# Summing both parts of the attention scores in PSUM as 128-column products, with one clip on VectorE

## The reference

```python
q = (lat @ Wq).reshape(b, n, HEADS, DHEAD).transpose(0, 2, 1, 3)
k, v = jnp.split(ctx @ Wkv, 2, axis=-1)
k = apply_rope(k, cos[None, None], sin[None, None])
attn = jnp.einsum('bhnd,bhsd->bhns', q, k) * DHEAD ** (-0.5)
attn = jnp.clip(attn, -11.0, 11.0)
attn = jax.nn.softmax(attn, axis=-1)
out = jnp.einsum('bhns,bhsd->bhnd', attn, v)
```

## Time and profile before

| | us |
|---|---|
| median of 3 runs | 1478.19 (1476.39 to 1479.28) |
| the profiled execution | 1474.36 |
| its span | 1472.6 |
| TensorE busy | 1385.8 (94%) |
| VectorE, ScalarE, GpSimd busy | 849.3, 792.9, 844.1 |

### The profile page before, as it was taken

One profiled execution on the slowest core, in us unless ns is written; L12 is line 12 of the kernel. 1 busy time (PEld: TensorE's weight loads), 2 busy tenths in 40 slices (PEclk: granted clock), 3 DMA queues, 4 the chain that ended last, 5 costly groups with the idle time before them and its releaser, 6 DMA issues. The chain is left out here.

```text
span 1472.6 us, 25163 instructions
## 1 busy us (share of the span) xinstructions
PE 1385.8 (94%) x8732; PEld 1137.1 (77%) x8732; DVE 849.3 (58%) x1417; ACT 792.9 (54%) x1224; POOL 844.1 (57%) x727
## 2 busy tenths in 40 slices
PE   4899999999999999999999999999995899999993
PEld 2578888888888888878888888888885576866662
DVE  7366665666556566656665666565553456665552
ACT  2346566656566666656566656666554212445650
POOL 3457777766677777767677767777665233200002
PEclk9999999999999999999999999999996899899997
DMA  6567666766667766657666766667566650569983
GB/s 209 205 108 133 122 119 111 131 116 135 123 108 128 118 129 112 132 109 125 122 117 128 116 134 120 122 117 119 88 103 147 231 213 0 195 241 360 359 322 107
DMA packets 115236, 218.44 MB, mean 148 GB/s; under 512 B 13328, under 2 KB 49168, under 8 KB 108944
## 3 DMA queue, kind: packets, MB, share of 16 engines
q1 hardware_dynamic: 111648, 208.48, 63.2%
q0 software_dynamic: 1280, 4.20, 0.9%
q10 hardware_dynamic: 2160, 3.93, 0.7%
HBM read 132.67 MB, written 16.78 MB: 101 GB/s over the span
## 5 line engine op out<-in xcount | busy, mean ns | idle before, releaser
L572 POOL TENSOR_TENSOR p_parts<-probs,p_parts 128x512 fp32r<-128x512 f32 x256 | 340.2, 1348 | 249.2 <-ACT p_parts L610 249.1
L610 ACT ACTIVATE p_parts<-probs 128x512 fp32r<-128x512 f32 x256 | 147.8, 625 | 244.3 <-PE ps_o L838 235.8
L706 DVE TENSOR_TENSOR probs<-ps_s,probs 128x1024 f32<-128x1024 f32 x128 | 156.7, 1224 | 156.7 <-ACT probs L616 156.7
L651 ACT ACTIVATE probs<-probs 128x1024 f32<-128x1024 f32 x128 | 135.9, 1061 | 145.0 <-POOL probs L579 144.6
L790 PE MATMUL ps_v<-wv_hi,x_hi 128*128 128x512 f32 x512 | 208.3, 407 | 3.6 <-PEq L169 3.6
L791 PE MATMUL ps_v<-wv_lo,x_hi 128*128 128x512 f32 x512 | 202.7, 396 | 0.0
L805 PE MATMUL ps_k<-x_hi,wk_hi 128*128 128x512 f32 x512 | 202.0, 394 | 0.0
L792 PE MATMUL ps_v<-wv_hi,x_lo 128*128 128x512 f32 x512 | 201.8, 394 | 0.0
L807 PE MATMUL ps_k<-x_hi,wk_lo 128*128 128x512 f32 x512 | 199.6, 390 | 0.0
L806 PE MATMUL ps_k<-x_lo,wk_hi 128*128 128x512 f32 x512 | 199.3, 389 | 0.0
L834 PE MATMUL ps_o<-p_parts,v_hi 128*65 128x128 f32 x1024 | 195.5, 226 | 1.6 <-POOL p_parts L572 1.6
(11 more groups left out here) (253 smaller groups left out, 2678.4 us busy)
## 6 DMA issues: line engine op xcount, KB each, us to landing
queries<-q_scratch SPq DMA_DIRECT2D x256, 128.0 KB, 6.0
keys<-wo_room SPq DMA_DIRECT2D x128, 256.0 KB, 5.6
keys<-turned_odd SPq DMA_DIRECT2D x128, 256.0 KB, 5.6
row_room<-in_ctx SPq DMA_DIRECT2D x64, 256.0 KB, 6.2
down<-in_down SPq DMA_DIRECT2D x10, 1024.0 KB, 7.5
wo_room<-in_gate SPq DMA_DIRECT2D x8, 1024.0 KB, 8.3
gate_raw<-in_up SPq DMA_DIRECT2D x8, 1024.0 KB, 10.0
up_raw<-in_gate SPq DMA_DIRECT2D x7, 1024.0 KB, 8.8
```

The lines of the kernel that those rows point to most:

```text
L572: nc.gpsimd.tensor_tensor(p_parts[:, 1, j, :], probs[:, pair % 2, j, :], p_parts[:, 0, j, :].bitcast(F32), ALU.subtract).then_inc(p_lo_rea ...
L706: nc.vector.tensor_tensor(mine, ps_s[:, :, :, 0, :].rearrange("p j i n -> p (j i) n"), mine, ALU.add).then_inc(s_taken, 1)
```

## The change

`score` has 16 products in place of 8. Each has 128 columns, one part of the query, and the two parts of a tile go one after the other into the same place of PSUM (`start` on the first, `stop` on the second), so that PSUM holds the whole score. The key tile is the weight of both. What a pair needs in PSUM falls to two banks, and `ps_s` becomes two buffers of two banks.

ScalarE's copy and GpSimd's clip are gone. VectorE reads the score from PSUM, clips it and writes it to `probs` in one instruction, which waits for `s_ready` and for the low parts that last read that buffer (`p_lo_ready`, a wait which the copy on ScalarE had). The exponential waits for `s_taken`. `score` waits for the `s_taken` of two pairs before, and the transposes of `turn_sums` go into the buffer that the step's scores don't use.

```diff
...
@@ -426,13 +426,17 @@
 
 
 
-        ps_s = psum("ps_s", [P, 2, ROW_TILES, 2, QUERIES])
+        ps_s = psum("ps_s", [P, 2, 2, ROW_TILES, QUERIES])
         ps_v = psum("ps_v", [P, 2, 512])
         ps_k = psum("ps_k", [P, 512])
         ps_o = psum("ps_o", [P, 512])
         sums = ps_o[0:DHEAD + 1, 0:2 * QUERIES].rearrange("p (j n) -> p j n", n=QUERIES)
         rows["ps_tr"] = ps_o[:].rearrange("p (t n) -> p t n", n=P)
-        turned_sums = ps_s[:, 0, 0:2, 0, 0:DHEAD + 1]
+
+        def turned_sums(pair):
+
+            return ps_s[:, (pair + 1) % 2, 0, 0:2, 0:DHEAD + 1]
+
 
         v_ready = sem("v_ready")
         v_hi_ready = sem("v_hi_ready")
...
@@ -572,15 +574,8 @@
                         nc.gpsimd.tensor_tensor(p_parts[:, 1, j, :], probs[:, pair % 2, j, :], p_parts[:, 0, j, :].bitcast(F32),
                                                 ALU.subtract).then_inc(p_lo_ready, 1)
 
-            def clip(b, pair):
-                if exists(b, pair):
-                    wait_alone(pool, s_taken, b * BSTEPS + (pair + 1))
-                    mine = probs[:, pair % 2]
-                    nc.gpsimd.tensor_scalar(mine, mine, CLIP / SCALE, -CLIP / SCALE, ALU.min, ALU.max).then_inc(clipped, 1)
-
             def step(b, t):
                 low_probs(b, t - VALUE_LAG)
-                clip(b, t - SCORE_LAG)
                 if t % 2 == 0 and exists(b, t - 2):
                     group = b * GROUPS + (t // 2 - 1)
                     slot = (t // 2 - 1) % 2
...
@@ -609,14 +604,6 @@
                     for j in range(2):
                         nc.scalar.activation(p_parts[:, 0, j, :], probs[:, pair % 2, j, :], ACT.Copy).then_inc(p_hi_ready, 1)
 
-                pair = t - SCORE_LAG
-                if exists(b, pair):
-                    wait(act, s_ready, b * BSTEPS + (pair + 1))
-                    wait(act, p_lo_ready, b * (2 * BSTEPS) + (2 * pair - 2))
-                    nc.scalar.activation(probs[:, pair % 2].rearrange("p j (i n) -> p (j i) n", n=P),
-                                         ps_s[:, :, :, 1, :].rearrange("p j i n -> p (j i) n"),
-                                         ACT.Copy).then_inc(s_copied, 1)
-
                 if exists(b, t - 1):
                     p = (t - 1) % STEPS
                     wait(act, v_ready, b * BSTEPS + t)
...
@@ -647,7 +634,7 @@
 
                 pair = t - SCORE_LAG
                 if exists(b, pair):
-                    wait(act, clipped, b * BSTEPS + (pair + 1))
+                    wait(act, s_taken, b * BSTEPS + (pair + 1))
                     nc.scalar.activation(probs[:, pair % 2], probs[:, pair % 2], ACT.Exp, scale=SCALE).then_inc(probs_ready, 1)
                 rope_high(1)
                 tile = row_tile_of(b, t - 1)
...
@@ -701,10 +688,12 @@
 
             def take_scores(b, pair):
                 if exists(b, pair):
-                    wait(dve, s_copied, b * BSTEPS + (pair + 1))
-                    mine = probs[:, pair % 2].rearrange("p j (i n) -> p (j i) n", n=P)
-                    nc.vector.tensor_tensor(mine, ps_s[:, :, :, 0, :].rearrange("p j i n -> p (j i) n"), mine,
-                                            ALU.add).then_inc(s_taken, 1)
+                    wait(dve, s_ready, b * BSTEPS + (pair + 1))
+
+                    wait(dve, p_lo_ready, b * (2 * BSTEPS) + (2 * pair - 2))
+                    nc.vector.tensor_scalar(probs[:, pair % 2].rearrange("p j n -> p (j n)"),
+                                            ps_s[:, pair % 2].rearrange("p j i n -> p (j i n)"),
+                                            CLIP / SCALE, -CLIP / SCALE, ALU.min, ALU.max).then_inc(s_taken, 1)
 
             def values_low(b, t):
                 if exists(b, t):
...
@@ -725,11 +714,11 @@
                         wait(dve, attn_ready, done)
                     if m >= 2 and not last_batch(b, pair):
                         wait(dve, attn_stored[m % 2], 16 * (STORES * whose + m // 2))
-                    nc.vector.reciprocal(recip[:], turned_sums[:, :, DHEAD]).then_inc(recip_ready, 1)
+                    nc.vector.reciprocal(recip[:], turned_sums(pair)[:, :, DHEAD]).then_inc(recip_ready, 1)
                     wait(dve, recip_ready, done + 1)
                     there = keep["attn_last"][:, m * P:(m + 1) * P] if last_batch(b, pair) else attn[:, m % 2, :]
                     for j in range(2):
-                        out = nc.vector.tensor_scalar(there[:, j * DHEAD:(j + 1) * DHEAD], turned_sums[:, j, 0:DHEAD],
+                        out = nc.vector.tensor_scalar(there[:, j * DHEAD:(j + 1) * DHEAD], turned_sums(pair)[:, j, 0:DHEAD],
                                                       recip[:, j:j + 1], None, ALU.mult)
                     out.then_inc(attn_ready, 1)
 
...
@@ -764,15 +753,16 @@
                     slot = pair // 2 % 2
                     wait(pe, keys_landed[slot], 64 * (b * (BSTEPS // 4) + pair // 4 + 1))
                     wait(pe, q_landed[pair % QUERY_SLOTS], 32 * (b * (BSTEPS // QUERY_SLOTS) + (pair // QUERY_SLOTS + 1)))
-                    wait(pe, s_taken, b * BSTEPS + pair)
+                    wait(pe, s_taken, b * BSTEPS + pair - 1)
                     done = pair - 3
                     if ends_batch(b, done):
 
                         wait(pe, attn_ready, PAIRS * (b + done // BSTEPS) + (done % STEPS + 1))
                     for j in range(2):
                         for i in range(ROW_TILES):
-                            mm = nc.tensor.matmul(ps_s[:, j, i], keys[:, slot, 2 * (pair % 2) + j, i * P:(i + 1) * P],
-                                                  queries[:, pair % QUERY_SLOTS, j], start=True, stop=True)
+                            for part in range(2):
+                                mm = nc.tensor.matmul(ps_s[:, pair % 2, j, i], keys[:, slot, 2 * (pair % 2) + j, i * P:(i + 1) * P],
+                                                      queries[:, pair % QUERY_SLOTS, j, part], start=(part == 0), stop=(part == 1))
                     mm.then_inc(s_ready, 1)
 
             def values(b, t, ks):
...
@@ -811,10 +801,10 @@
                 if ends_batch(b, pair):
                     wait(pe, o_added, b * BSTEPS + (pair + 1))
 
-                    if exists(b, pair + 2):
-                        wait(pe, s_taken, b * BSTEPS + (pair + 3))
+                    if exists(b, pair + 1):
+                        wait(pe, s_taken, b * BSTEPS + (pair + 2))
                     for j in range(2):
-                        tr = nc.tensor.transpose(turned_sums[:, j, :], acc[:, 2 * (pair % STEPS) + j, :],
+                        tr = nc.tensor.transpose(turned_sums(pair)[:, j, :], acc[:, 2 * (pair % STEPS) + j, :],
                                                  keep["ident"][0:DHEAD + 1, 0:DHEAD + 1])
                     tr.then_inc(o_turned, 1)
```

More of the change, by code:

```diff
@@ L447, in attend @@
         s_ready = sem("s_ready")
-        s_copied = sem("s_copied")
         s_taken = sem("s_taken")
-        clipped = sem("clipped")
         probs_ready = sem("probs_ready")
```

## The result

The changed kernel takes 1576.33 us (median of 4, 1575.22 to 1578.52) against 1477.48 for the kernel before in the same set. The ratio is 1.0659, with a 95% interval from 1.0634 to 1.0685: some 99 us slower. The profiled execution took 1575.95 us with a span of 1574.2, 101.6 more than the span before.

What follows compares the result with a forecast made beforehand. TensorE's issue was taken to bound the steps: 124 pairs x 0.86 = +106.6 us, less 1.7 and 0.7 at the end, gives +104.2, 1578.6 for the profiled execution and 1582 for a median; range 1566 to 1608.

Steps and rivals of the forecast that it cites:

- TensorE bounds the steps: Steady attention steps: a step costs what TensorE issues, 7.92 us; work taken off ScalarE and GpSimd is worth 0.
- There is one load for each product: Score products: each loads its weight even when the tile repeats, so loads go from 8 to 16 a pair.
- the router's row: Score products: 0.113 us apart, just over the router products' 0.112; 16 take 1.808 us, +0.86 us a pair.
- The weighing's 0.060: Products weighing the values: their 0.060 us distance, with weights 64 or 65 columns wide, says nothing of 128-wide loads.
- The end: Attention's last four pairs, where the chain through all engines shows: terms of -1.7 and -0.7 us.
- The last stretch: From the last pair's scores at 1138.19, lower clock: eight more loads +1.8, transposes' wait -2.46, together -0.7 us.
- The stretch between: From 1125.74 to 1138.19, in the last four pairs: set by the last query pair's DMA, unchanged.
- The first stretch of the end: From 1110.93 to 1125.74, until the last keys land: scores +0.86, copy -1.03, GpSimd's clip -1.54, together -1.7 us.
- No new wait appears: Attention's end: the last exponential ends about when the weighing of the pair before does, so no wait is added.
- the free second load: Rival, score products: a tile's second load costs nothing, distance 0.060 us, 1475 us in all, faster; chance 0.09.
- the partial overlap: Rival, score products: load and product overlap partly, distance 0.086 us, +53 us over 124 pairs, 1528 us; chance 0.07.
- one after the other: Rival, score products: load and product do not overlap, distance 0.172 us, +223 us, about 1700 us; chance 0.04.

Runs made afterwards that it cites:

- the relief alone: Kernel before with ScalarE's copy and GpSimd's clip taken out, VectorE clipping from PSUM, the query's second part multiplied but not added: 1471.07 us, ratio 0.9965.
- Putting the parts apart: Changed kernel with its 16 score products reordered, four tiles with the query's first part, then four with the second: 1578.31 us, ratio 1.0680.
- the runs with 64 and 32 weight columns: Changed kernel with the second part's product loading only 64 or 32 of the key tile's 128 columns: 1525.62 us and 1522.42 us.
- the products alone: Kernel before, copy, addition and GpSimd clip kept, each 256-column score product split into two of 128 written to separate places: 1581.94 us, ratio 1.0710.
- the short stream: Changed kernel with the second part's product streaming 32 columns instead of 128 against the full key tile: 1579.16 us, ratio 1.0679.
- one part left out: Changed kernel without the products of the query's second part, 8 products of 128 columns a pair: 1464.69 us, ratio 0.9906.

## Why the prediction was right

The forecast was 1582 us, +104.2; measured were 1576.33 and +101.6 in the span of the profiled execution, +98.9 by the medians. Of the 5.7 us between the two times, 2.6 are the sum's. The other 3 come from the last term: the forecast took the median to lie 3.8 us above the profiled execution, as it did before, and it lay 0.4 above it. Single executions differ by that much, and nothing in the runs supports the term. By its steps:

- *TensorE bounds the steps, and relief of the others is worth nothing there.* Right: TensorE has no idle time from 430 to 700 us after, and the run with the relief alone gains 0.012 us a pair.
- *There is one load for each product, also for a repeated tile.* Right: 9756 of both. Putting the parts apart changes nothing.
- *The distance of two products is that of the router's row.* Right, and 0.113 was a little dear: the single starts lie 0.111 (products) to 0.112 (loads) apart. With 0.1115 between them, 16 x 0.1115 = 1.784, less 0.948 is 0.836, which is what the trace gives for a pair over 124 pairs. The allowance for fp32r on top of the router's distance was not needed: 128 columns of it stream at the distance that the router's 8 columns had. The 0.024 us too much for a pair makes 3 us, which is most of what the forecast was above the measured span.
- *The weighing's 0.060 says nothing of wide loads.* This choice decided the case. The runs with 64 and 32 weight columns show it: 0.06 behind a load of 64 columns, 0.06 behind one of 32, 0.11 behind one of 128.
- *The end.* In all it is -2.9 for -2.4, and the two terms of the sum are not right in the same way. The last stretch was put at -0.7 and measured, 14.50 against 13.60, at -0.9, by the mechanism forecast: the products alone lengthen it by 1.7 (16.22), and 2.6 come back in the changed kernel, where the transposes no longer wait (2.46 before). Its load distance was read a little too long: the last load lasts 0.33 at the lower clock and not the 0.19 that was subtracted, and single starts lie 0.214 apart where the forecast had 0.227. The stretch between, which a DMA paces, is 12.45 and 12.33.
- *The first stretch of the end* was put at -1.7 and measured, 14.81 against 12.96, at -1.85, but this is partly luck. The path that was added up (longer scores +0.86, copy -1.03, clip -1.54) sets the stretch before the change. After it ScalarE is done earlier than GpSimd, which works without a gap from the low parts of the probabilities to the low parts of the last keys:

```profile
1215.90 2.64 POOL L574 TENSOR_TENSOR p_parts<-probs,p_parts 128x512 fp32r<-128x512 f32 x2 [6.43 <-ACT p_parts L605]
...
1218.49 2.97 POOL L586 TENSOR_TENSOR turned_odd<-turned_odd 128x512 fp32r<-128x512 f32 x2
```

Its end lies 6.53 us behind the start of the pair's scores, where it was 8.06, and the keys land 6.4 us later in place of 6.8. So the longer scores cost nothing here: the relief alone, with its 8 products, has the same stretch, 12.95 us.
- *No new wait appears.* Wrong in one place: the second of the last four scores now waits 0.9 us for VectorE's division of the transposed sums. The relief alone, with one buffer, has the same 0.9 us, so the two buffers are not its cause. The division begins 4.7 us behind the start of the pair's scores before and after; what changed is that TensorE is ready for it sooner. The wait is hidden by the DMA that comes after.
- *The clip from PSUM costs VectorE what the addition cost.* Right: 1225 ns against 1224.
- *ScalarE 128 us and GpSimd 153 us less busy.* 124 and 137. GpSimd's rotation of the keys became longer, below.

Of the rivals, the free second load was refuted by the measured 0.111 itself and by the narrow weights, which show what a second load that hides would give; the partial overlap by the same 0.111 in every run with 128-wide loads and 128 columns or fewer; one after the other by the short stream, in which 96 columns less change nothing. The Trainium skill (TensorE: Matmul & The Clock Gate, "Back-to-back issue gap") has 81 ns for a product of 128 columns in a stream of loads and products; this kernel's float32 loads give 111.

The clock at the end, on which one term rests: at the lower level, 0.50 granted from 1240 to 1245 us, the 16 loads take 3.49 us where the 8 took 1.78.

```profile
1240.18 3.49 PEld L764 LDWEIGHTS ps_s<-queries,keys 128*128 128x128 f32 x16 [6.06 <-issue]
...
1243.90 1.23 DVE L694 TENSOR_SCALAR probs<-ps_s 128x1024 f32<-128x1024 f32 x1 [9.18 <-PE ps_s L764]
```

## What to carry to other kernels

Count weight loads as well as columns: here a 128 x 128 float32 load took 0.11 us at the full clock, about as long as 256 columns take to stream (0.1185 us a product before the change), so a product of 128 columns against a full tile pays for 256, whatever is done with its result. Columns that stream against a tile already being loaded are nearly free up to that point, so two parts that share a weight belong in one product, even when another engine must add them up, as long as that engine has the time. Work moved off engines that wait for TensorE gives its time back only where TensorE itself runs dry, here in the last four of 128 pairs.

## What the runs showed of the hardware

In this kernel VectorE's additions and GpSimd's subtractions hold each other up when both work on SBUF. The rotation's second addition on VectorE (the same instruction, SBUF to SBUF) and GpSimd's subtraction of the rotated keys became longer after the change; before, in the first two rows, after, in the last two:

```profile
L688 DVE TENSOR_TENSOR wo_room<-wo_room 128x512 f32<-128x512 f32 x32 | 22.1, 691 | 0.0
L591 POOL TENSOR_TENSOR wo_room<-wo_room 128x512 fp32r<-128x512 f32 x64 | 82.8, 1294 | 32.0 <-ACT wo_room L635 32.0
```

```profile
L675 DVE TENSOR_TENSOR wo_room<-wo_room 128x512 f32<-128x512 f32 x32 | 31.2, 975 | 0.0
L586 POOL TENSOR_TENSOR wo_room<-wo_room 128x512 fp32r<-128x512 f32 x64 | 95.5, 1514 | 17.6 <-ACT wo_room L622 17.6
```

The relief alone shows it most plainly. VectorE's addition starts while a GpSimd subtraction runs, and GpSimd's next one starts while the addition runs:

```profile
1109.08 2.63 POOL L572 TENSOR_TENSOR p_parts<-probs,p_parts 128x512 fp32r<-128x512 f32 x2 [5.57 <-ACT p_parts L609]
...
1110.45 1.81 DVE L679 TENSOR_TENSOR turned_odd<-turned_odd 128x512 f32<-128x512 f32 x1
...
1111.66 1.74 POOL L590 TENSOR_TENSOR turned_odd<-turned_odd 128x512 fp32r<-128x512 f32 x1
```

The addition, 0.68 us by itself, ends 0.55 us after the first subtraction does (1112.26 against 1111.71); the second subtraction, 1.27 us by itself, takes 1.74. In the changed kernel 61 of the 64 such additions start while a subtraction runs, and each lasts 0.55 us plus what is left of it, within 0.01. With one part left out the addition starts 0.07 us before one subtraction ends and 0.03 us before the next starts (1109.13 and 1109.16); it keeps its 0.68 us, and that next subtraction takes 1.79. By these lengths whichever of the two is first runs to its end and the other waits for it. GpSimd's clip, which reads one operand, does not do this: before the change the addition overlaps it by 0.44 us on average and takes 0.69.

With the copy and the clip gone, VectorE comes to this addition while GpSimd is still at the low parts of the probabilities. In the steady steps that cost nothing, as both engines wait anyway. In the first stretch of the end, which GpSimd paces, its first subtraction of the last keys takes 1.73 us in place of 1.27.
